# Attention on one core: folded row maximum, 512-column products, masked copies by VectorE and ScalarE

## The reference, cut to what matters

```
q, k = rope(x @ wqr + bqr), rope(x @ wkr + bkr)      # B=16, N=256, 16 heads of 8
v    = gelu(x @ wkv + bkv) @ wv + bv
s    = q @ k.T / sqrt(8), with s[i, j] = -inf for j > i
out  = softmax(s) @ v;  y = x2 + gate * (out @ wo + bo)
```

## Time and profile before

| | us |
|---|---|
| median of 3 runs | 2268.09 |
| profiled execution | 2270.32 |
| its span | 2268.5 |
| PE busy | 1792.7 (79%) |
| DVE busy | 1521.5 (67%) |
| ACT busy | 1079.4 (48%) |
| POOL busy | 899.3 (40%) |

### The profile page before, as it was taken

How to read it: one execution, slowest core, us unless ns; L and a number is a source line. 1 busy time by engine, 2 the same in 40 slices (tenths; PEclk the granted TensorE clock), 3 DMA queues, 4 the chain that set the end, 5 groups by cost and what they waited for, 6 DMA issues and landing times. The chain is left out here.

```text
span 2268.5 us, 35662 instructions
## 1 busy us (share of the span) xinstructions
PE 1792.7 (79%) x10242; PEld 1367.0 (60%) x10242; DVE 1521.5 (67%) x4241; ACT 1079.4 (48%) x1795; POOL 899.3 (40%) x729
## 2 busy tenths in 40 slices
PE   3285986858768587776852998989999899999998
PEld 2153654535545364454522887878888777777776
DVE  3299989989999999999983444444544434444442
ACT  1264564636646365464531545545454344443333
POOL 1777787776877777877960000000000000000000
PEclk8597898978989789888985999999999799999999
DMA  5420020200102011020005111101101000000000
GB/s 91 86 52 1 6 57 1 62 1 18 44 1 61 1 29 33 0 57 1 10 5 125 20 24 25 19 14 22 24 6 43 15 15 14 9 12 14 14 14 12
DMA packets 140822, 59.92 MB, mean 26 GB/s; under 512 B 94600, under 2 KB 135037, under 8 KB 140669
## 3 DMA queue, kind: packets, MB, share of 16 engines
q1 hardware_dynamic: 140668, 58.24, 11.5%
HBM read 37.10 MB, written 21.10 MB: 26 GB/s over the span
## 5 line engine op out<-in xcount | busy, mean ns | idle before, releaser
L594 PE MATMUL pb<-hid,wd 128*128 128x512 f32 x528 | 303.4, 660 | 196.3 <-POOL hid L406 195.5
L402 POOL TENSOR_TENSOR hid<-act_g,act_u 128x512 f32<-128x512 f32 x256 | 328.9, 1285 | 163.7 <-ACT act_c L518 148.0
L406 POOL TENSOR_TENSOR hid<-hid,act_c 128x512 f32<-128x512 f32 x256 | 329.0, 1285 | 20.6 <-POOL hid L402 1.0
L518 ACT ACTIVATE act_g<-pb 128x512 f32<-128x512 f32 (+1 forms) x264 | 158.1, 599 | 373.8 <-PE pb L545 332.7
L1345 PE MATMUL l_pb<-l_xt,l_big 128*128 128x512 f32 (+1 forms) x1024 | 299.3, 414 | 35.1 <-DVE l_rope L1624 24.6
L1692 DVE SCALAR_TENSOR_TENSOR l_acc<-l_pb,l_gtok,l_acc 128x128 f32<-128x128 f32 x512 | 144.5, 344 | 258.2 <-PE l_pb L1345 257.9
L543 PE MATMUL pb<-xt_hi,wg_hi 128*128 128x512 f32 (+1 forms) x264 | 189.1, 716 | 90.6 <-ACT act_g L518 90.6
L1273 ACT ACTIVATE l_hid<-l_pb,l_cols 128x512 f32<-128x512 f32 x256 | 169.4, 688 | 183.0 <-PE l_pb L1345 182.7
L1345 PEld LDWEIGHTS l_pb<-l_big,l_hid 128*128 128x128 f32 x2048 | 247.1, 192 | 10.5
L594 PEld LDWEIGHTS pb<-hid,wd 128*128 128x128 f32 x528 | 101.4, 206 | 250.8 <-POOL hid L406 224.6
L1734 DVE TENSOR_REDUCE l_mrow<-l_pb 128x2 f32<-128x256 f32 (+1 forms) x256 | 137.2, 555 | 171.7 <-PE l_pb L1345 168.7
(11 more groups left out here) (309 smaller groups left out, 4125.5 us busy)
## 6 DMA issues: line engine op xcount, KB each, us to landing
z_scratch<-zs SPq DMA_DIRECT2D x128, 81.0 KB, 3.0
zr<-z_scratch SPq DMA_DIRECT2D x8, 1296.0 KB, 8.0
x_sb<-in_L_attn_x_dram SPq DMA_DIRECT2D x32, 64.0 KB, 2.1
g_scratch<-zs SPq DMA_DIRECT2D x8, 256.0 KB, 2.8
y_scratch<-yo SPq DMA_DIRECT2D x8, 256.0 KB, 2.1
l_xs<-in_L_attn_x_dram SPq DMA_DIRECT2D x32, 64.0 KB, 1.9
l_ys<-y_scratch SPq DMA_DIRECT2D x128, 16.0 KB, 1.8
l_gs<-g_scratch SPq DMA_DIRECT2D x8, 256.0 KB, 3.0
```

The costliest lines, as they stand in the source:

```text
L402: pool.tensor_tensor(hid1[:, :], g, u, ALU.mult).then_inc(s_h1, 1)
L406: pool.tensor_tensor(hid[:, (p + par) % 2, :], hid1[:, :], c, ALU.mult).then_inc(s_h, 1)
L518: act.activation(dst, pb[0:n, what, :], ACT.Silu if what == 0 else ACT.Copy).then_inc(s_ev, 1)
L594: last = pe.matmul(pb[:, SUM, :], wd[0:n, p, :], hid[0:n, (p + par) % 2, :], start=(p == 0), stop=(p == PAIRS), skip_group_check=True)
```

## The change

- Maxima: the query side is no longer masked but copied once (qr, by VectorE), and the keys are masked instead (kb, 16 heads, by VectorE: masked_keys, 8 instructions of 512 elements, at units 1, 5 and 7). So one product can have several heads side by side in its 512 columns. There are 12 units: for each group of four heads one with the first half of the queries (4 heads x 128 keys) and two with the second half (2 heads x 256 keys), each followed by one mask product of 512 or 256 columns. They use banks 2 and 3. VectorE reduces 512 elements each time.
- The maximum is folded into the scores' product: two of the 32 rows of each head are spare. kspare (a bias in ScalarE's copy of k) puts -1 there, and the transposed maxima are written into the same rows of the masked queries qb. So esel and mT go, with their products.
- The masked queries for scores_t are written by ScalarE out of SBUF (masked_queries, 8 instructions of 512 elements, at units 4, 7, 10 and 13).
- The transposed maxima: mhl has 32 columns for a head, so that eight transposes put each head's two rows at the partitions 32 j. They go to banks 2 and 3. ScalarE copies them for j = 0 and 1, VectorE for j = 2 and 3, each with two instructions of 2 partitions x 1024 elements.
- scores_t is now two products for a pair of heads (512 and 256 columns), without mask, in one pair of banks (4 and 5) where there were two. Each waits for the exponential before it. The eight pairs are placed at the units 3, 4, 6, 7, 9, 10, 12, 13, and values at 9, 11, 14, 17.
- The causal mask after the exponential is GpSimd's: for each pair of heads a small multiplication (turn, one element) and two affine_select of 2 x 128 elements. values waits for them (s_cut). GpSimd had nothing to do in the attention before.
- pt2 holds the second four probabilities, so a whole batch of them has room.

```diff
-        esel = sb("esel", [P, H1, P], F32R)
+        kb = sb("kb", [P, H1, N], F32R)
+        pt2 = sb("pt2", [P, 4, 3 * N])
-        mhl = sb("mhl", [P, 2, P], F32R)
-        mT = [sb(f"mT{i}", [P, N], F32R) for i in range(2)]
+        mhl = sb("mhl", [P, 2, H1, 32], F32R)
...
-        UNITS = ["k"] * 2 + ["q_dve", "q_act"] + ["max0"] * 8 + ["max1"] * 8 + ["v", "mT"]
+        UNITS = ["k0", "q0", "k1", "q1"] + ["max"] * 12 + ["v", "m"]
+        BANK = {0: 0, 1: 1, 2: 0, 3: 1, 16: 0, 17: 0}
...
+        QUERIES_AT, KEYS_AT = {4: (0, 0), 7: (0, 2), 10: (1, 0), 13: (1, 2)}, {1: (0, 0, 4), 5: (1, 0, 2), 7: (1, 2, 2)}
+        X_AT, V_AT = (3, 4, 6, 7, 9, 10, 12, 13), (9, 11, 14, 17)
...
+        O_RAW, O_TB, O_NORM, O_OT, O_WO, O_END = 0, 1, 2, 4, 6, 7
...
+            def causal(b, u, turns):
+                pool.wait_ge(s_pt, b * XU + u + 1)
+                turn(turns)
+                for k in range(2):
+                    diagonal = probs(u)[k][:, :, 0:P]
+                    last = pool.affine_select(diagonal, diagonal, pattern=[[0, 2], [1, P]], base=0, channel_multiplier=-1,
+                                              compare_op=ALU.is_ge, fill=0.0)
+                last.then_inc(s_cut, 1)
...
+                elif u == "m":
+                    act.wait_ge(s_ua, b * NU + (i + 1))
+                    act.wait_ge(s_qb, (b + 1) * 4)
+                    for j in range(2):
+                        last = act.activation(max_rows(par, j), pb[32 * j:32 * j + 2, 2:4, :].rearrange("p a (g n) -> p (a g) n", n=N), ACT.Copy)
+                    last.then_inc(s_mq[0], 1)
...
+            def masked_queries(b, par, i):
+                half, first = QUERIES_AT[i]
+                act.wait_ge(*read(b, 2 * half + 1))
+                for j in range(first, first + 2):
+                    at = slice(2 * N * half, 2 * N * (half + 1))
+                    dst = qb[par][:, 8 * half:8 * (half + 1), :].rearrange("p (g j) n -> p g j n", j=4)[:, :, j, :]
+                    last = act.activation(dst, qr[:, at].rearrange("p (g n) -> p g n", n=N).bitcast(F32), ACT.Copy, scale=qmask[:, j:j + 1])
+                last.then_inc(s_qb, 1)
...
+                    if part == 0:
+                        mm(bank.rearrange("p (j n) -> p j n", j=4), qr[:, N * g:N * g + P], kb[:, 4 * g:4 * (g + 1), 0:P], stop=False)
+                        last = mm(bank.rearrange("p (j n) -> p j n", j=4), ident_b[:, :], mask_b[:, :].unsqueeze(1).to_broadcast([P, 4, P]), start=False)
+                    else:
+                        h = 4 * g + 2 * (part - 1)
+                        mm(bank, qr[:, N * g + P:N * (g + 1)], kb[:, h:h + 2, :].rearrange("p h n -> p (h n)"), stop=False)
+                        last = mm(bank.rearrange("p (j n) -> p j n", j=2)[:, :, P:N], ident_b[:, :], mask_b[:, :].unsqueeze(1).to_broadcast([P, 2, P]), start=False)
...
             def scores_t(b, par, u):
                 if u == 0:
-                    pe.wait_ge(s_ua_act, (b + 1) * N_ACT)
-                    pe.wait_ge(s_pt, b * XU)
-                elif u >= 2:
-                    pe.wait_ge(s_pt, b * XU + (u - 1))
-                bank = 512 * (2 + 2 * (u % 2))
-                for k, m, lo in ((1, 1, N), (1, 0, P), (0, 0, 2 * N), (0, 1, 3 * N)):
...
-                    mm(out, kr[par][:, keys:keys + P], qb[par][:, h, :], stop=False)
-                    mm(out, esel[:, h, :], mT[par][:, :], start=False, stop=False)
-                    last = mm(out[:, P * k:P * (k + 1)], mask_b[:, :], ident_b[:, :], start=False)
+                    for n in range(2):
+                        pe.wait_ge(s_mq[n], b + 1)
+                pe.wait_ge(s_pt, b * XU + u)
+                g, heads = u // 2, slice(2 * u, 2 * u + 2)
+                mm(pb[:, 4, :], kr[par][:, N * g:N * g + P], qb[par][:, heads, :].rearrange("p h n -> p (h n)"))
+                last = mm(pb[:, 5, 0:N].rearrange("p (m n) -> p m n", m=2), kr[par][:, N * g + P:N * (g + 1)], qb[par][:, heads, P:N])
...
+            def masked_keys(b, par, i):
+                half, first, n = KEYS_AT[i]
+                dve.wait_ge(*read(b, 2 * half))
+                for j in range(first, first + n):
+                    at = slice(2 * N * half, 2 * N * (half + 1))
+                    dst = kb[:, 8 * half:8 * (half + 1), :].rearrange("p (g j) n -> p g j n", j=4)[:, :, j, :]
+                    last = dve.tensor_scalar(dst, kr[par][:, at].rearrange("p (g n) -> p g n", n=N).bitcast(F32), qmask[:, j:j + 1], None, ALU.mult)
+                last.then_inc(s_kb, 1)
```

More of the change, by code:

```diff
@@ L1101, in _ @@
             w(qmask[:, :], d["c_qmask"])
+            w(kspare[:, :], d["c_kspare"])
             w(rope[:, 1, 0:P], d["c_mask"])
@@ L1218, in _, with turn, batch @@
                 pool.memset(vp[i][:, :, :, HD1:HD1 + 1], 1.0).then_inc(s_init, 1)
+            pool.memset(turnstile[:, :], 0.0).then_inc(s_turn, 1)
+            def turn(n):
+                pool.wait_ge(s_turn, n)
+                pool.tensor_tensor(turnstile[:, 1:2], turnstile[:, 0:1], turnstile[:, 0:1], ALU.mult).then_inc(s_turn, 1)
+            def causal(b, u, turns):
[6 more added lines that the diff above has]
+                last.then_inc(s_cut, 1)
+            pool.wait_ge(s_kv, NT)
+            def batch(b, turns):
+                for u in range(XU):
+                    causal(b, u, turns + u)
+            with pool.Fori(0, B) as b:
+                batch(b, b * XU + 1)
         @block.scalar
@@ L1286, in a_unit @@
             def a_unit(b, par, i):
+                u = UNITS[i]
                 if i == 0:
                     act.activation(ckv_b[0:DC1 + 1, :], ckvT[0:DC1 + 1, bass.ds(b, 1), :].rearrange("p o n -> p (o n)"), ACT.Copy).then_inc(s_ckb, 1)
[L1289 to L1301, removed]
-                                   ACT.Copy).then_inc(s_ua_act, 1)
-                else:
-                    act.activation(mT[par][:, :], src[:, 0:N], ACT.Copy).then_inc(s_ua_act, 1)
@@ new lines, in a_unit @@
+                bank = pb[:, BANK[i], :]
+                if u == "m":
+                    pe.wait_ge(s_mhl, b + 1)
+                    for h in range(0, H1, 4):
+                        for k in range(2):
+                            src = mhl[:, k, h:h + 4, :].rearrange("p j c -> p (j c)").bitcast(F32)
+                            at = 2 * 512 + N * (h // 4) + P * k
+                            last = pe.transpose(pbf[:, at:at + P], src, ident[:, :])
+                    last.then_inc(s_ua, 1)
+                    return
@@ L1724, in a_unit @@
                 dve.wait_ge(s_ua, b * NU + (i + 1))
-                if u == "q_dve":
-                    for g in range(2):
-                        q = src[:, N * g:N * (g + 1)].unsqueeze(1).to_broadcast([P, 4, N])
-                        last = dve.tensor_tensor(qb[par][:, 4 * g:4 * (g + 1), :], q, over(qmask[:, :], N), ALU.mult)
-                    last.then_inc(s_ua_dve, 1)
-                    return
-                j, k = i - UNITS.index(u), int(u[3])
-                src = src.rearrange("p (h n) -> p h n", h=2)[:, :, 0:P * (k + 1)]
@@ L1819, in constants @@
                 for i in range(HD1):
-                    rep[h * HD1 + i, kind, h // 4, 32 * (h % 4) + HD1 * part + i] = 1
+                    rep[h * HD1 + i, kind, h // 4, 32 * (h % 4) + HD1 * (part + 1) + i] = 1
     c["c_rep"] = rep.reshape(P, -1)
-    esel = np.zeros((P // H1, H1, H1, P), f)
-    for h in range(H1):
-        esel[0:2, h, h, :] = -1
-    c["c_esel"] = esel.reshape(P, -1)
+    spare = np.zeros((4, 32), f)
+    spare[:, 0:2] = -1
+    c["c_kspare"] = spare.reshape(P, 1)
     return c
```

175 lines of the change are left out of this document (108 added, 67 removed).

## The result

The changed kernel takes **2169.12 us** (median of 4 runs, 2166.51 to 2169.51) against 2268.09: ratio 0.9566, 95% interval 0.9549 to 0.9583. The forecast was 2173. The profiled executions are 2270.32 and 2166.51: 103.8 us less, of which 3.5 lie ahead of the attention, which starts at 1756.6 instead of 1760.1 us, and 100.3 in the attention. Of the 3.5, about 1 us is there at the first tile of layer 1 (POOL's first ql starts at 1255.7 against 1256.7), so it comes from layer 0, which the change doesn't touch; for most of the rest the clock stayed up in the last expert tiles (1.00 over 1690 to 1760, 0.98 before).

What follows compares the result with a forecast made beforehand. PE's product stream was taken to bound the attention, then a loop through four engines. First batch 19.0, second round 24.2, 14 rounds 338.8 and end 27.0 make 409.0 us, 97 less: 2173 us, range 2142 to 2255.

Steps and rivals of the forecast that it cites:

- PE was the bound before, and the products fall out: Attention rounds: PE's product stream sets the time before; after the change its sum is 17.6 us, no longer the bound alone.
- The others' sums: Work of the other engines in an attention round after the change: ACT 16.8 us, DVE 16.6, POOL 8.4.
- The loop: New bound of an attention round: a chain through four engines, from the maxima's transposes to the two parts, 23.4 us.
- The waits of the reductions: Among a round's maxima, DVE waits for PE because scores wait for the previous exponential: 3.0 us, bounds 0 and 6.
- The clock: PE idles some 2.7 us in each attention round, so its clock falls in most rounds, costing 0.8 us a round.
- The end: Last stretch of the attention: 27.0 us, some 3 us longer, since eight scores and exponentials are strictly in turn.
- First batch and second round: Start of the attention: 19.0 us for the first batch, which starts cold, and 24.2 us for the second round.
- Sum: All attention stretches together: 409.0 us after against 506.1 before, 97 us less, giving 2173 us for the kernel.
- Dear or held keys: VectorE's masked keys run at one element a cycle (2208 us) or are held up by POOL (2198 us); chance 0.15.
- POOL's mask: Attention: affine_select is so dear that values wait for POOL, 2287 us, or some 2225 if less dear; chance 0.11.
- The clock that never rises: PE stays at half clock in the attention, 30.5 us a round, 2271 us in all; chance 0.08.
- Two signs that I named: Attention: a mean clock of 0.75 to 0.9, and a wait chain passing DVE and ACT for over half a round.

Runs made afterwards that it cites:

- the first experiment: The kernel before the change, without its 32 esel products in a round, so the maximum is not subtracted from the scores: 2217.93 us, ratio to before 0.9786.
- The ninth experiment: The changed kernel with the scores of pairs 3, 5 and 7 in banks 0 and 1 instead of 4 and 5: 2161.37 us.
- experiments 8 and 10: The changed kernel with ScalarE's raw output copy ahead of its maxima copies, 2139.04 us; the same plus scores of pairs 3, 5, 7 in banks 0 and 1, 2129.87.
- the fifth: The changed kernel with each mask product of the maxima done twice: 2185.10 us, ratio to the kernel before 0.9659.

## Why the prediction was right, point by point

- **PE was the bound before, and the products fall out.** Shown by the first experiment, and by the loop that came in its place. How the 99 us divide over the parts of the change is not shown, but for esel's 48.5. By starts in the round above, a maximum of four heads takes 0.55 and one of two 0.38, 5.2 us in all (forecast 5.5), a pair of scores 0.43, 3.5 in all (2.9), the values 0.79 four times, 3.2 (3.6); with the rest PE's sum is 17.4 (17.6).
- **The others' sums** were 16.6 for DVE and 16.8 for ACT. The windows have 234.15 / 14 = 16.7 and 225.43 / 14 = 16.1. A masked key cost 0.41 us (0.38, bounds 0.34 to 0.68), an affine_select 0.39 in a pair (0.45, bounds 0.32 to 1.3), POOL's round 7.6 (8.4). The nearest row was in both cases the right guide. The pair with the small multiplication is 0.96 (1.05).
- **The loop** was 23.4 us; it is 23.6 where the clock holds. Link by link: transposes 1.0, 1.21; ACT 3.06, 3.14; transposes and q0 1.74, 1.70; DVE up to the reductions 3.70, 4.06 with a wait of 0.41; reductions with all between them 13.05, 13.0; the parts 0.4, 0.5. The forecast's terms add up to 23.45 us, and its 0.5 for hand-overs lies among the measured links. The idle piece was put at 2.7 us and is 2.79.
- **The waits of the reductions: right in size, wrong in most of the cause.** Forecast 3.0 us; 42.6 / 14 = 3.04. But I put them down to scores that wait for an exponential. In the round above the waits are five: 0.93 us behind such scores, twice 0.65 behind the values, 0.41 ahead of the first reduction, where the first maximum stands behind the transposes of the normalised output, and 0.38, most of which stays when the exponentials' waits go. The ninth experiment takes three of the four exponential waits away: the reductions then wait 2.0 us in a round, and the round is 0.7 shorter. So about a third of the term is the exponentials'; the values, which the forecast did not name, are more, 1.3 us. (Only three of the four pairs of scores have a maximum between them; the first has q1.) The agreement in size is luck, and the expectation of the ninth, built on the same reason, failed.
- **The clock: it does fall behind the idle piece, but far less often.** "I expect it to fall in most rounds" was wrong for this kernel: three of 14. A fall costs 1.3 us rather than 0.8, so the term is 0.3 instead of 0.8 us in a round. That, with a loop 0.2 longer, is the difference between 24.2 and 23.89, 4.4 us over 14 rounds.
- **The end** was put at 27.0 and took 29.2. The eight exponentials are strictly in turn, as said, 1.51 apart at full clock; but the clock was low for most of the first 12 us, and there they are 1.9 apart. ACT, and the two windows:

```profile
2139.32 0.81 ACT L1369 ACTIVATE l_big<-l_pb 128x768 f32<-128x768 f32 x1 [2.70 <-PE l_pb L1406]
2141.23 0.81 ACT L1369 ACTIVATE l_big<-l_pb 128x768 f32<-128x768 f32 x1 [1.09 <-PE l_pb L1406]
...
2150.03 0.81 ACT L1369 ACTIVATE l_pt<-l_pb 128x768 f32<-128x768 f32 x1 [0.70 <-PE l_pb L1406]
```
```profile
2133.20:2145.20 12.00, 7.37 (x29) 5.78 (x26) 3.65 (x6) 5.76 (x7) 2.71 (x9) 0.58 0.01 1
2145.20:2164.80 19.60, 10.55 (x92) 6.39 (x90) 2.19 (x7) 5.46 (x7) 4.52 (x15) 0.76 0.04 14
```

- **First batch and second round** 18.5 and 23.7 (19.0, 24.2).
- **Sum**: 405.8 in the attention against 409.0, and 3.5 us ahead of it that no step had. That 2169 comes so near 2173 is in part errors that cancel: rounds and first batches came out shorter, the end longer.
- **What the rivals were worth.** *Dear or held keys* did not come, but VectorE and GpSimd do hold each other up. Where two keys were under way when the selects came (1904.97), the keys took 0.87 us and the pair of selects 0.96; where the selects were first (1907.42), they took 0.76 and the keys 1.02; the small multiplication took 0.46 beside the keys and 0.19 elsewhere. That is a few tenths in a round, not 1.8. The Trainium skill, "SBUF — State Buffer", section "Who interferes with whom", says that with VectorE in a two-port mode the engine that issues first has the shared ports for its whole instruction, and the other waits. These rows agree on who waits, with delays of 0.15 to 0.27 us, less than one instruction of 0.4; that the keys run in such a mode is shown by no run. *POOL's mask* costs 0.5 us a round at twice its cost and the whole gain at three times. *The clock that never rises* did not come: of the 14 rounds 11 were at 1.00 throughout. In the round from 1868.68 it was down for the output's transposes (1.97 us), and by the first maximum (1879.25) the products were back at their full pace.
- **Two signs that I named did not show as named.** The mean clock is 0.97 in the rounds and 0.94 over the whole attention, above the 0.75 to 0.9 forecast, which follows from the fewer falls. And the chain of waits gave most of this stretch as "issue", so it could not show DVE and ACT for half of a round; the timelines did.

## What to carry to other kernels

When the bound engine is relieved by more than the next one has room, write down the loop from one round to its successor, link by link with each queue's order, not only the engines' sums: here no engine is over 80% busy, the sums stop at 17.6 us, and the loop is 23.6. Then look for the link that only stands in the wrong order: one copy moved ahead of two others gave 30 us more, without any work taken away. An agreement in size doesn't prove the cause of a term; take away the cause by itself before building on it.

## What the runs showed of the hardware that was not expected

- The clock's falls make costs jump. The same 1.9 us of VectorE work cost 1.9 us in one round and 5.4 in the next, in which the clock fell twice (0.59, 0.84, 0.50 in 4 us windows), though PE's two idle pieces are about as long in both (2.79 and 2.55, 2.79 and 2.2).
- Among the 14 rounds of each kernel here, the clock fell only in rounds with an idle piece of PE of 1.5 us or more. With the 2.79 us piece filled down to 0.87, 14 rounds with their small waits (0.35, 0.67 and 0.54 in the unfilled kernel) showed no fall. The Trainium skill, "TensorE: Matmul & The Clock Gate", section "A second HAM failure mode: psum-queue depth-cycling", tells of a kernel whose clock swung because TensorE idled in small pieces; no round here shows that from pieces under 1.5 us. At 1.54 us (experiments 8 and 10) it fell in 2 and 5 rounds of 14, and with this piece filled in none.
- Products that compute nothing, put where the engine would wait anyway, bought 3.5 to 7 us, of which the rounds show 4. Why a piece of 2.79 us brings the clock down in one round and not in another stays open: it did so in 3 of 14 rounds of the changed kernel, in 10 of the ninth and in 11 of the fifth, which wait the same 2.79 us.
